# Delta-rule block with a routed expert layer, one core: the gate's columns inside the experts' operand, products of a pair in three parts, and other list orders in the last stage

## Chip, cores and metric

The kernel runs on one NeuronCore of a Trainium2 chip. The metric is the device time of one execution in microseconds, lower is better. Three executions of the kernel before took 234.13, 236.33 and 236.86 us, median 236.33.

## The reference

The input x is 4 x 1024 x 128 in float32. The program adds two sublayers to it, each on a layer-normalised copy of x:

```python
# sublayer 1, on layernorm(x): delta rule over the 1024 positions, then an MLP
qkv = x @ gates_w + gates_b; q, k, v = split(qkv, 3); k = k / norm(k)
u = solve_triangular(tril(k k^T, -1) + I, v); y = (q k^T) @ (lr * u)
h = x + y @ out_w + out_b
h = h + relu(layernorm(h) @ w1 + b1) @ w2 + b2
# sublayer 2, on layernorm(x1): one of 8 experts a row, by the largest score
scores = x @ gate_w.T; chosen = argmax(scores)        # 8 scores a row
x = x + expert_w[chosen] @ x                           # expert_w: 8 x 128 x 128
```

The normalisation ahead of sublayer 2 is folded into the operands: gate and expert weights are centred once, so that they can be applied to x1 itself, and the factor 1/std of each row is applied to the chosen result afterwards. The scores of a row differ from the true ones only by that positive factor, which changes no argmax.

## The kernel before, in words

Positions are cut into T = 8 tiles of 128 rows; each tile holds all NS = 4 sequences. Each engine has one program-ordered list, and semaphores join them. The first two thirds of the span compute k, v, the triangular solve and the state; the last stage, from about 125 us on, goes through the tiles once more with the state known. The change is nearly all in this stage. For a tile t its steps are:

- `delta` (TensorE) multiplies q's operand with the state into PSUM bank 0; `h2_` (VectorE) adds it to h; `xb_` (GpSimd) adds h to x; `hstats`, `haggr` (VectorE: one statistics and one aggregate instruction a sequence), `hroot` (ScalarE, square root), `hscale`, `hbias` (VectorE) give the normalisation; `tn_` (ScalarE, four instructions) applies it.
- `tT_`, `hid_`, `out_` (TensorE, banks 1, 2, 2) with their evacuations `tT_` and `hid_` on ScalarE are the MLP; `x1_` (VectorE) adds its result to x.
- `x1T_` transposes the sum (TensorE, bank 1) and evacuates it (ScalarE). `gate` multiplies each transposed block with the 8 centred score columns `gwC` into bank 3: four matmuls of 8 columns. `choose` (VectorE) takes the maximum of the 8 scores and compares, which makes the mask, for four sequences at once.
- `experts(t, pair, half)` (TensorE) multiplies the blocks of a pair of sequences with four experts, 512 columns of `ewC`, one bank a sequence: half 0 (experts 0 to 3) goes to banks 4 and 5, half 1 to 6 and 7. `default` (ScalarE) copies expert 0's result to `sel`. Seven `pick`s (VectorE, predicated copies of 128 x 256) put experts 1 to 7 in place where the mask says so; each waits for the one before it. A bank is written anew only when the picks that read it are over: half 0 of a pair waits for three picks of the pair before, half 1 for all seven.
- `xstats`, `xaggr`, `xroot`, `xscale` give 1/std of the sum; `scale` (ScalarE) applies it, `add_` (GpSimd) adds the result to x, and SP's queue stores the tile. For the last tile VectorE does the last scaling and adding itself (line 1039).

The lists at the end of each engine's block order all this by hand: while tile t's experts are picked, tile t + 1 is in its MLP, t + 2 in its normalisation and t + 3 in delta. `prep` (lines 427 to 438 and 1091 to 1105) and `expert_` and `expert_one` (1108 to 1115) centre the gate's and the experts' weights during the earlier stages, through bank 4. A float32 matmul shows as two passes in the profile: "x4" for the two matmuls of `experts`.

Of the kernel before, what the change touches and what calls it, by code (L numbers as in the profile page):

```python
# [5 lines left out]
P = 128  # L6
# [3 lines left out]
ALU = mybir.AluOpType  # L10
# [7 lines left out]
def delta_block_kernel(  # L18
# [44 lines left out]
    with ExitStack() as ctx:  # L63
        def sb(name, shape, dtype=F32):
            return ctx.enter_context(nc.sbuf_tensor(name, shape, dtype))

        def sem(name):
            return ctx.enter_context(nc.semaphore(name))
# [6 lines left out]
        def rows(t):  # L75
# [111 lines left out]
        x1T_mm, x1T_ready, gate_mm, max_done, mask_ready = (sem("x1T_mm"), sem("x1T_ready"), sem("gate_mm"),  # L187
                                                            sem("max_done"), sem("mask_ready"))
# [13 lines left out]
        AHEAD = 1  # L202

# [145 lines left out]
        def _(act):  # L349
# [77 lines left out]
            def prep(j):  # L427
                act.wait_ge(prep_mm, j + 1)
                if j == 0:
                    nc.scalar.copy(wqT[:], ps[:, 4, 0:C])  # L430
                    last = nc.scalar.copy(gwT[:], ps[:, 4, C:C + E])
                elif j == 3:
                    last = nc.scalar.copy(gwC[:], ps[:, 4, 0:E])
                else:
                    q = (j - 1) % 3
                    last = nc.scalar.copy((ewT if j < 3 else ewC)[:, EH * q:EH * q + EH, :].rearrange("p e f -> p (e f)"),
                                          ps[:, 4, :])
                last.then_inc(prep_ready, 1)
# [219 lines left out]
            for t in range(T):  # L658
                if 0 < t < T - 1:
                    tT_(t + 1)  # L660
                if t + 2 < T:
                    tn_(t + 2, LOW)
                default(t, 0)
                if t + 1 < T:
                    hid_(t + 1)
                if t + 2 < T:
                    tn_(t + 2, HIGH)
                if t > 0:
                    scale(t - 1)
                xroot(t)  # L670
                default(t, 1)
                if t + 1 < T:
                    x1T_(t + 1)
                if t + 3 < T:
                    hroot(t + 3)

        @block.vector
        def _(dve):
# [267 lines left out]
            def choose(t, of=ALL):  # L946

                scores = ps[:, 3, 0:NS * E].rearrange("p (n e) -> p n e", n=NS)[:, span(of)]
                dve.wait_ge(gate_mm, upto(t, of))
                nc.vector.tensor_reduce(mx[t % 2][:, span(of)], scores, AX_X, ALU.max).then_inc(max_done, len(of))  # L950
                dve.wait_ge(max_done, upto(t, of))
                nc.vector.tensor_tensor(mask[t % 2][:, span(of)], scores,
                                        mx[t % 2][:, span(of)].unsqueeze(2).broadcast_to([P, len(of), E]),
                                        ALU.is_equal).then_inc(mask_ready, len(of))

            def pick(t, pair, j):

                e = j + 1
                half = e // EH
                b = 4 + 2 * half  # L960
                n = slice(2 * pair, 2 * pair + 2)
                if j == 0:
                    dve.wait_ge(mask_ready, NS * t + 2 * pair + 2)
                    dve.wait_ge(default_set, 2 * t + pair + 1)
                else:
                    dve.wait_ge(picked, (E - 1) * (2 * t + pair) + j)
                if j == 0 or e == EH:
                    dve.wait_ge(ex_mm, 4 * t + 2 * pair + half + 1)
                nc.vector.copy_predicated(  # L969
                    sel[t % 2][:, n], mask[t % 2][:, n, E - 1 - e].unsqueeze(2).broadcast_to([P, 2, F]),  # L970
                    ps[:, b:b + 2, (e % EH) * F:(e % EH) * F + F]).then_inc(picked, 1)
# [19 lines left out]
            choose(0, LOW)  # L991
            hstats(2)
            haggr(2)
            choose(0, HIGH)
            for t in range(T):
# [3 lines left out]
                if t > 0:  # L999
                    choose(t)  # L1000
# [12 lines left out]
                if far:  # L1013
                    hstats(t + 3, LOW)
# [30 lines left out]
        def _(pe):  # L1045
# [265 lines left out]
            def gate(t, of=ALL):  # L1311
                pe.wait_ge(x1T_ready, upto(t, of))
                earlier(pe, mask_ready, NS * t + of[0])
                for n in of:
                    last = nc.tensor.matmul(ps[:, 3, n * E:n * E + E], x1T[t % 2][:, n], gwC[:], start=True, stop=True)  # L1315
                last.then_inc(gate_mm, len(of))

            def experts(t, pair, half):
                i = 2 * t + pair
                pe.wait_ge(x1T_ready, NS * t + 2 * pair + 2)  # L1320

                earlier(pe, picked, (E - 1) * i - (EH if half == 0 else 0))
                for n in range(2):
                    last = nc.tensor.matmul(ps[:, 4 + 2 * half + n, :], x1T[t % 2][:, 2 * pair + n],  # L1324
                                            ewC[:, EH * half:EH * half + EH, :].rearrange("p e f -> p (e f)"),
                                            start=True, stop=True)
                last.then_inc(ex_mm, 1)
# [60 lines left out]
```

## Time and profile before

| | |
|---|---|
| runs | 234.13, 236.33, 236.86 us |
| profiled execution | 233.88 us, span 232.1 us |
| TensorE (PE) | 203.6 us busy, 88% |
| VectorE (DVE) | 164.5 us, 71% |
| ScalarE (ACT) | 122.8 us, 53% |
| GpSimd (POOL) | 58.9 us, 25% |
| line 1324, the experts' matmuls | 128 passes, 60.4 us busy |
| line 969, the picks | 112 instructions, 48.9 us busy |
| line 1315, the gate's matmuls | 64 passes |

The span is the time from the first to the last instruction; the execution's own time is a little longer. Busy time is that of one engine, and passes of matmuls overlap in it, so that the spacing of their starts says more than their durations. PEld is the loading of the stationary operand, which overlaps the matmul before it. PEclk is the granted TensorE clock as a share of 2.4 GHz. The last stage ends at 232.1; its tile steps are 11.4 us apart in the middle and 10.3 towards the end.

### The profile page before, as it was taken

The page shows a single profiled execution, that of the slowest core. Times are in us where ns is not written, and L with a number is a line of the kernel's source. Part 1 is how long each engine was busy: PE and PEld are TensorE (multiplying, and loading weights), DVE is VectorE, ACT ScalarE, POOL GpSimd, SP SyncE. Part 2 cuts the span into 40 slices and gives each one's busy share as a digit, 9 for nine tenths or more (in the row PEclk, how much of TensorE's full clock was granted, in tenths as well). Part 3 has the DMA queues.
Part 4 walks back from the last instruction along what each step waited for, and adds up shares of the span by engine and source line. Part 5 has one row for each costly group of instructions (what it writes and reads, how often), then busy time and mean ns, then how long its engine had stood idle before and what let it go on. Part 6 is the DMA issues. An engine that isn't in the chain of part 4 may idle for free.

```text
span 232.1 us, 4284 instructions
## 1 busy us (share of the span) xinstructions
PE 203.6 (88%) x1347; PEld 146.6 (63%) x1347; DVE 164.5 (71%) x748; ACT 122.8 (53%) x324; POOL 58.9 (25%) x73
## 2 busy tenths in 40 slices
PE   0795988999999759999989498999999999999980
PEld 0454666977799658989987285565656565565520
DVE  7994999999489854142353825969696878787785
ACT  2585565789585652434672555354646373735130
POOL 7255800000000069740200402206060606022020
PEclk9999799999999975557999859999999999999998
DMA  5951011000000000000000000001010101010111
GB/s 137 265 138 26 3 24 21 6 3 0 3 4 0 3 0 0 4 0 0 4 0 3 1 0 0 0 3 47 0 45 1 48 1 45 0 45 3 45 47 45
DMA packets 15612, 5.92 MB, mean 26 GB/s; under 512 B 5468, under 2 KB 15590, under 8 KB 15590
## 3 DMA queue, kind: packets, MB, share of 16 engines
q1 hardware_dynamic: 15014, 5.58, 9.6%
q8 instruction: 11, 0.18, 0.3%
q10 hardware_dynamic: 576, 0.07, 0.2%
q14 instruction: 11, 0.09, 0.1%
HBM read 3.09 MB, written 2.10 MB: 22 GB/s over the span
## 4 chain that ended last, share of the span: by engine, by line
PE 72%; DVE 8%; ACT 5%; issue 3%; DVEq 0%; ACTq 0%
PE ps L1324 22%; PE ps L1053 8%; PE ps L1048 5%; PE ps L1220 4%; PE ps L1224 4%; PE ps L1214 4%; PE ps L1232 3%; PE ps L1080 3%; PE ps L1299 3%; PE ps L1315 3%; PE ps L1150 2%; PE ps L1160 2%; DVE kT_all L969 2%; PE ps L1124 2%; ACT tt_all L448 1%
## 5 line engine op out<-in xcount | busy, mean ns | idle before, releaser
L1324 PE MATMUL ps<-ewC,kT_all 128*128 128x512 f32 x128 | 60.4, 596 | 0.9 <-DVE kT_all L969 0.8
L969 DVE COPY_PREDICATED kT_all<-mask,ps 128x256 f32<-128x256 int32 x112 | 48.9, 436 | 17.2 <-ACT kT_all L634 11.1
L1324 PEld LDWEIGHTS ps<-ewC,kT_all 128*128 128x128 f32 x128 | 22.0, 190 | 19.2 <-issue 19.2
L315 POOL TENSOR_SCALAR h_all<-x_all,mv,rr 128x128 f32<-128x128 f32 x16 | 12.4, 790 | 54.9 <-DVE da_all L817 54.9
L333 POOL TENSOR_TENSOR x_all<-x_all,kT_all 128x512 f32<-128x512 f32 x7 | 8.9, 1270 | 55.4 <-ACT kT_all L640 55.4
L789 DVE TENSOR_TENSOR xi<-xi,prod 128x60 f32<-128x60 f32 (+13 forms) x116 | 19.5, 207 | 0.3
L782 DVE TENSOR_TENSOR prod<-lts,xi 128x60 f32<-128x60 f32 (+13 forms) x116 | 19.3, 206 | 0.3
L328 POOL TENSOR_TENSOR x_all<-x_all,h_all 128x512 f32<-128x512 f32 (+1 forms) x9 | 10.3, 1147 | 30.9 <-DVE h_all L900 24.1
L611 ACT ACTIVATE k_all<-h_all,nb,rr 128x128 f32<-128x128 f32 x32 | 14.0, 484 | 4.2 <-DVE nb L921 4.2
L839 DVE SCALAR_TENSOR_TENSOR rv<-v_all,nk,ps 128x128 f32<-128x128 f32 x28 | 8.4, 345 | 10.0 <-PE ps L1214 9.5
L1048 PE MATMUL ps<-ident,h_all 128*128 128x128 f32 x32 | 6.0, 320 | 9.4 <-ACT h_all L363 7.0
L634 ACT COPY kT_all<-ps 128x256 f32<-128x256 f32 x16 | 5.8, 363 | 15.6 <-PE ps L1324 15.6
L1048 PEld LDWEIGHTS ps<-ident,h_all 128*128 128x128 f32 x32 | 4.7, 168 | 14.9 <-issue 14.6
L299 POOL TENSOR_SCALAR h_all<-x_all,mv,rr 128x128 f32<-128x128 f32 x14 | 11.1, 804 | 10.6 <-DVE rr L710 10.6
L322 POOL TENSOR_TENSOR x_all<-x_all,b2s 128x512 f32<-128x512 f32 x8 | 10.1, 1268 | 12.0 <-ACT h_all L527 12.0
L1220 PE MATMUL ps<-rv,tt_all 128*128 128x128 f32 x64 | 10.9, 323 | 1.4 <-DVE tt_all L832 0.6
L1053 PE MATMUL ps<-kT_all 128*128 128x128 f32 x64 | 9.9, 303 | 2.3 <-ACT kT_all L372 2.3
L1053 PEld LDWEIGHTS ps<-w2s,k_all 128*128 128x128 f32 x64 | 9.2, 208 | 4.0 <-issue 3.3
L1053 PEld LDWEIGHTS ps<-kT_all 128*128 128x128 f32 x64 | 8.4, 205 | 4.5 <-ACT kT_all L372 4.4
L1053 PEld LDWEIGHTS ps<-gg_all,xnT_all 128*128 128x128 f32 x64 | 9.1, 209 | 3.0 <-issue 2.4
L1220 PEld LDWEIGHTS ps<-rv,tt_all 128*128 128x128 f32 x64 | 9.4, 225 | 2.1 <-DVE rv L839 1.4
L1315 PEld LDWEIGHTS ps<-gwC,kT_all 128*128 128x128 f32 x64 | 8.5, 193 | 3.3 <-issue 3.3
(160 smaller groups left out, 437.4 us busy)
## 6 DMA issues: line engine op xcount, KB each, us to landing
x_all<-in_L_attn_x_dram SPq DMA_DIRECT2D x7, 256.0 KB, 5.5
out_dram<-x_all SPq DMA_DIRECT2D x7, 256.0 KB, 2.3
ew<-in_L_ffn_expert_w_dram SPq DMA_DIRECT2D x1, 512.0 KB
gd<-gg_all SPq DMA_DIRECT2D x28, 16.0 KB, 1.8
x_all<-in_L_attn_x_dram SPq DMA_DIRECT2D x2, 128.0 KB, 2.6
out_dram<-x_all SPq DMA_DIRECT2D x2, 128.0 KB, 1.8
wall<-in_L_attn_gates_w_dram SPq DMA_DIRECT2D x2, 64.0 KB
wall<-in_L_attn_gates_w_dram ACTq DMA_DIRECT2D x1, 64.0 KB, 2.6
```

The source lines that it names most:

```text
L299: nc.gpsimd.tensor_scalar(xh[:, t, n], x_all[:, t, n], mv[:, 0, t, n, 0:1], rr[:, t, 1, n:n + 1], ALU.subtract, ALU.mult).then_inc(xh_pool, 1)
L315: last = nc.gpsimd.tensor_scalar(h_all[:, t, n], x_all[:, t, n], mv[:, 0, t, n, 0:1], rr[:, t, 0, n:n + 1], ALU.subtract, ALU.mult)
L328: nc.gpsimd.tensor_tensor(x_all[:, t, span(of)], x_all[:, t, span(of)], h_all[:, t, span(of)], ALU.add).then_inc(xb_ready, len(of))
L611: nc.scalar.activation(tn[t % 2][:, n], h_all[:, t, n], ACT.Identity, bias=nb2[:, t, n:n + 1], scale=rr2[:, 0, t, n:n + 1]).then_inc(tn_re ...
L782: nc.vector.tensor_tensor(mul[half], lts[:, j, lo:hi].unsqueeze(2).broadcast_to([P, hi - lo, w]), xi[g][:, j, 0:w].unsqueeze(1).broadcast_ ...
L789: nc.vector.tensor_tensor(xi[g][:, lo:hi, 0:w], xi[g][:, lo:hi, 0:w], mul[half], ALU.subtract).then_inc(elim, 1)
L969: nc.vector.copy_predicated(sel[t % 2][:, n], mask[t % 2][:, n, E - 1 - e].unsqueeze(2).broadcast_to([P, 2, F]), ps[:, b:b + 2, (e % EH) * ...
L1048: last = nc.tensor.transpose(tiles(bank)[:, n], src(n), ident[:])
L1053: last = nc.tensor.matmul(tiles(bank)[:, n], lhsT(n), rhs(n), start=True, stop=True)
L1220: nc.tensor.matmul(ps[:, n, C:2 * C], tt_all[:, t, n], rv[:, n], start=True, stop=True).then_inc(w_mm, 1)
L1315: last = nc.tensor.matmul(ps[:, 3, n * E:n * E + E], x1T[t % 2][:, n], gwC[:], start=True, stop=True)
L1324: last = nc.tensor.matmul(ps[:, 4 + 2 * half + n, :], x1T[t % 2][:, 2 * pair + n], ewC[:, EH * half:EH * half + EH, :].rearrange("p e f -> ...
```

## The change

`gwC` is gone. `ewC` is now one row of 8 x 128 + 8 columns: experts 0 and 1, the 8 score columns, experts 2 to 7. A pair's products come in three parts of 256, 392 and 384 columns (`COLS`). Part 0 puts both sequences side by side in bank 3; part 1, with the scores, goes to banks 4 and 5; part 2 to 6 and 7. The matmuls `gate` are removed; `choose` works on a pair and waits for part 1, twice a tile. The waits of `experts` follow the picks that free each bank: 1, 4 or 7 of the pair before. In `prep`, the centred weights are evacuated to their new places, one of them in two copies. The lists of the stage are reordered:

- TensorE: tT_, part 0, hid_, part 1, delta, part 2, out_, then the second pair's parts 0 and 1, x1T_, part 2.
- ScalarE: default comes ahead of tn_, which is now one block of four behind hid_; hroot(t + 2) follows default(t, 0) instead of hroot(t + 3) at the end of the step.
- VectorE: hstats(t + 3) and haggr(t + 3), which stood between the picks, follow the last pick of the step.

```diff
-        gwT, gwC = sb("gwT", [P, E]), sb("gwC", [P, E])
+        gwT = sb("gwT", [P, E])
-        ewT, ewC = sb("ewT", [P, E, F]), sb("ewC", [P, E, F])
+        ewT, ewC = sb("ewT", [P, E, F]), sb("ewC", [P, E * F + E])
+        COLS = (slice(0, 2 * F), slice(2 * F, 5 * F + E), slice(5 * F + E, 8 * F + E))
...
+        def expert(e):
+            if e < 2:
+                return ps[:, 3, :].rearrange("p (n c) -> p n c", n=2)[:, :, e * F:e * F + F]
+            if e < 5:
+                return ps[:, 4:6, E + (e - 2) * F:E + (e - 1) * F]
+            return ps[:, 6:8, (e - 5) * F:(e - 4) * F]
...
@@ ScalarE: prep @@
-                    last = nc.scalar.copy(gwC[:], ps[:, 4, 0:E])
+                    last = nc.scalar.copy(ewC[:, 2 * F:2 * F + E], ps[:, 4, 0:E])
...
+                elif j == 4:
+                    nc.scalar.copy(ewC[:, 0:2 * F], ps[:, 4, 0:2 * F])
+                    last = nc.scalar.copy(ewC[:, 2 * F + E:4 * F + E], ps[:, 4, 2 * F:4 * F])
                 else:
...
+                    last = nc.scalar.copy(ewC[:, 4 * F + E:8 * F + E], ps[:, 4, :])
@@ ScalarE: default and the list @@
-                act.wait_ge(ex_mm, 4 * t + 2 * pair + 1)
+                i = 2 * t + pair
+                act.wait_ge(ex_mm, 3 * i + 1)
                 earlier(act, added, t - 1)
-                nc.scalar.copy(sel[t % 2][:, 2 * pair:2 * pair + 2], ps[:, 4:6, 0:F]).then_inc(default_set, 1)
+                nc.scalar.copy(sel[t % 2][:, 2 * pair:2 * pair + 2], expert(0)).then_inc(default_set, 1)
...
             for t in range(T):
                 if 0 < t < T - 1:
                     tT_(t + 1)
-                if t + 2 < T:
-                    tn_(t + 2, LOW)
                 default(t, 0)
+                if 0 < t < T - 2:
+                    hroot(t + 2)
                 if t + 1 < T:
                     hid_(t + 1)
                 if t + 2 < T:
-                    tn_(t + 2, HIGH)
+                    tn_(t + 2, ALL)
                 if t > 0:
                     scale(t - 1)
                 xroot(t)
                 default(t, 1)
                 if t + 1 < T:
                     x1T_(t + 1)
-                if t + 3 < T:
-                    hroot(t + 3)
@@ VectorE: choose, pick and the list @@
+            def choose(t, pair):
+                i = 2 * t + pair
+                of = slice(2 * pair, 2 * pair + 2)
+                scores = ps[:, 4:6, 0:E]
+                dve.wait_ge(ex_mm, 3 * i + 2)
+                nc.vector.tensor_reduce(mx[t % 2][:, of], scores, AX_X, ALU.max).then_inc(max_done, 1)
+                dve.wait_ge(max_done, i + 1)
+                nc.vector.tensor_tensor(mask[t % 2][:, of], scores, mx[t % 2][:, of].unsqueeze(2).broadcast_to([P, 2, E]),
+                                        ALU.is_equal).then_inc(mask_ready, 1)
...
-                if j == 0 or e == EH:
-                    dve.wait_ge(ex_mm, 4 * t + 2 * pair + half + 1)
+                if e == 5:
+                    dve.wait_ge(ex_mm, 3 * i + 3)
...
-                if t > 0:
-                    choose(t)
+                choose(t, 0)
                 if ahead:
                     hbias(t + 2)
                 pick(t, 0, 0)
...
                 pick(t, 0, 4)
-                if far:
-                    hstats(t + 3, LOW)
                 pick(t, 0, 5)
                 if nxt:
                     x1_(t + 1)
                 pick(t, 0, 6)
-                if far:
-                    hstats(t + 3, (2,))
+                choose(t, 1)
                 pick(t, 1, 0)
-                if far:
-                    hstats(t + 3, (3,))
                 pick(t, 1, 1)
-                if far:
-                    haggr(t + 3, LOW)
                 pick(t, 1, 2)
                 xscale(t)
                 pick(t, 1, 3)
-                if far:
-                    haggr(t + 3, HIGH)
                 pick(t, 1, 4)
                 pick(t, 1, 5)
                 pick(t, 1, 6)
+                if far:
+                    hstats(t + 3)
+                    haggr(t + 3)
@@ TensorE @@
-            def gate(t, of=ALL):
...
-            def experts(t, pair, half):
+            def experts(t, pair, third):
                 i = 2 * t + pair
                 pe.wait_ge(x1T_ready, NS * t + 2 * pair + 2)
-                earlier(pe, picked, (E - 1) * i - (EH if half == 0 else 0))
+                earlier(pe, picked, (E - 1) * (i - 1) + (1, 4, 7)[third])
+                of = COLS[third]
+                w = of.stop - of.start
                 for n in range(2):
-                    last = nc.tensor.matmul(ps[:, 4 + 2 * half + n, :], x1T[t % 2][:, 2 * pair + n],
...
+                    dst = ps[:, 3, n * w:n * w + w] if third == 0 else ps[:, 2 + 2 * third + n, 0:w]
+                    last = nc.tensor.matmul(dst, x1T[t % 2][:, 2 * pair + n], ewC[:, of], start=True, stop=True)
                 last.then_inc(ex_mm, 1)
...
             delta(2)
-            gate(0, LOW)
             x1T_(0, HIGH, 6)
             experts(0, 0, 0)
-            tT_(1)
-            gate(0, HIGH)
             for t in range(T):
-                if 0 < t < T - 1:
+                if t + 1 < T:
                     tT_(t + 1)
                 if t > 0:
                     experts(t, 0, 0)
                 if t + 1 < T:
                     hid_(t + 1)
+                experts(t, 0, 1)
                 if t + 3 < T:
                     delta(t + 3)
-                experts(t, 0, 1)
+                experts(t, 0, 2)
                 if t + 1 < T:
                     out_(t + 1)
                 experts(t, 1, 0)
+                experts(t, 1, 1)
                 if t + 1 < T:
                     x1T_(t + 1)
-                experts(t, 1, 1)
-                if t + 1 < T:
-                    gate(t + 1)
+                experts(t, 1, 2)
```

## Rows read from the trace of the kernel before

**Rows 1.** Busy time by stretch: engines, PEclk (granted clock), DMA share, GB/s.
```profile
85.00:96.90 11.90, 11.90 (x94) 10.80 (x92) 3.55 (x11) 3.20 (x11) 11.90 (x16) 0.50 0.00 0
152.21:163.57 11.36, 11.36 (x52) 6.82 (x52) 9.05 (x39) 6.09 (x15) 3.77 (x3) 1.00 0.09 25
218.35:232.10 13.75, 7.59 (x18) 2.77 (x17) 9.53 (x32) 2.21 (x7) 1.27 (x1) 0.95 0.14 39
```

**Rows 2.** The chain of waits, t = 2: start, us, what.
```profile
164.21 1.72 PE ps L1324 x4
165.93 0.86 PE ps L1299 x2
166.78 0.89 PE ps L1053 x8
...
174.29 0.79 PE ps L1315 x8
```

**Rows 3.** Timeline of TensorE: the transposes of four tiles at x1T_.
```profile
149.16 0.66 PE L1048 MATMUL ps<-ident,x_all 128*128 128x128 f32 x4 [0.32 <-DVE x_all L927]
...
194.62 0.65 PE L1048 MATMUL ps<-ident,x_all 128*128 128x128 f32 x4
...
205.05 0.60 PE L1048 MATMUL ps<-ident,x_all 128*128 128x128 f32 x4
...
215.39 0.60 PE L1048 MATMUL ps<-ident,x_all 128*128 128x128 f32 x4
```

**Rows 4.** Timeline of VectorE, t = 0 and 1: start, us, line, operation, idle.
```profile
139.83 0.86 DVE L906 BATCH_NORM_STATS2 st<-h_all 128x6 f32<-128x128 f32 x4
140.73 0.38 DVE L912 BATCH_NORM_AGGREGATE mv<-st 128x2 f32<-128x6 f32 x4
...
142.71 0.18 DVE L917 RECIPROCAL rr<-sd 128x4 f32<-128x4 f32 x1 [0.26 <-ACT sd L600]
...
153.53 0.16 DVE L950 TENSOR_REDUCE mx<-ps 128x4 f32<-128x32 f32 x1
153.79 0.19 DVE L952 TENSOR_TENSOR mask<-ps,mx 128x32 int32<-128x32 f32 x1
...
155.32 0.45 DVE L969 COPY_PREDICATED kT_all<-mask,ps 128x256 f32<-128x256 int32 x1 [1.26 <-ACT kT_all L634]
155.66 0.48 DVE L933 BATCH_NORM_STATS2 st<-x_all 128x6 f32<-128x128 f32 x2
156.05 0.43 DVE L969 COPY_PREDICATED kT_all<-mask,ps 128x256 f32<-128x256 int32 x1
...
158.48 0.37 DVE L939 BATCH_NORM_AGGREGATE mv<-st 128x2 f32<-128x6 f32 x4
...
159.79 0.68 DVE L927 TENSOR_TENSOR x_all<-ps,x_all 128x512 f32<-128x512 f32 x1
160.39 0.44 DVE L969 COPY_PREDICATED kT_all<-mask,ps 128x256 f32<-128x256 int32 x1
```

**Rows 5.** Timeline of ScalarE: an evacuation of ewC, and the stage's start.
```profile
59.23 0.59 ACT L436 COPY ewC<-ps 128x512 f32<-128x512 f32 x1
...
141.64 0.78 ACT L617 ACTIVATE k_all<-ps,cols 128x512 f32<-128x512 f32 x1 [1.79 <-PE ps L1048]
142.32 0.29 ACT L600 ACTIVATE sd<-mv,epsc 128x4 f32<-128x4 f32 x1
```

**Rows 6.** Timeline of TensorE and of VectorE round the first tile.
```profile
138.61 0.51 PE L1315 MATMUL ps<-gwC,kT_all 128*128 128x8 f32 x4
...
144.41 0.45 DVE L969 COPY_PREDICATED kT_all<-mask,ps 128x256 f32<-128x256 int32 x1 [1.26 <-ACT kT_all L634]
```

**Rows 7.** Timeline of VectorE, the end of the program.
```profile
220.81 0.44 DVE L969 COPY_PREDICATED kT_all<-mask,ps 128x256 f32<-128x256 int32 x1 [0.75 <-ACT kT_all L634]
...
226.93 1.87 DVE L969 COPY_PREDICATED kT_all<-mask,ps 128x256 f32<-128x256 int32 x4 [0.17 <-PE ps L1324]
228.69 1.13 DVE L1039 SCALAR_TENSOR_TENSOR x_all<-kT_all,rr,x_all 128x128 f32<-128x128 f32 x4
```

More of the change, by code:

```diff
@@ L186, in delta_block_kernel @@
         hid_mm, hid_ready, out_mm, x1_ready = sem("hid_mm"), sem("hid_ready"), sem("out_mm"), sem("x1_ready")
-        x1T_mm, x1T_ready, gate_mm, max_done, mask_ready = (sem("x1T_mm"), sem("x1T_ready"), sem("gate_mm"),
-                                                            sem("max_done"), sem("mask_ready"))
+        x1T_mm, x1T_ready, max_done, mask_ready = (sem("x1T_mm"), sem("x1T_ready"), sem("max_done"),
+                                                   sem("mask_ready"))
         xst_done, xmv_done, xsd_done, xrr_done = sem("xst_done"), sem("xmv_done"), sem("xsd_done"), sem("xrr_done")
@@ L432, in prep @@
                 elif j == 3:
-                    last = nc.scalar.copy(gwC[:], ps[:, 4, 0:E])
-                else:
-                    q = (j - 1) % 3
-                    last = nc.scalar.copy((ewT if j < 3 else ewC)[:, EH * q:EH * q + EH, :].rearrange("p e f -> p (e f)"),
-                                          ps[:, 4, :])
+                    last = nc.scalar.copy(ewC[:, 2 * F:2 * F + E], ps[:, 4, 0:E])
+                elif j < 3:
+                    last = nc.scalar.copy(ewT[:, EH * (j - 1):EH * j, :].rearrange("p e f -> p (e f)"), ps[:, 4, :])
+                elif j == 4:
+                    nc.scalar.copy(ewC[:, 0:2 * F], ps[:, 4, 0:2 * F])
+                    last = nc.scalar.copy(ewC[:, 2 * F + E:4 * F + E], ps[:, 4, 2 * F:4 * F])
+                else:
+                    last = nc.scalar.copy(ewC[:, 4 * F + E:8 * F + E], ps[:, 4, :])
                 last.then_inc(prep_ready, 1)
@@ L944, in xscale @@
                 nc.vector.reciprocal(rr2[:, 1, t], sd2[:, 1, t]).then_inc(xrr_done, 1)
[L946 to L954, printed above, removed]
+            def choose(t, pair):
[7 more added lines that the diff above has]
+                                        ALU.is_equal).then_inc(mask_ready, 1)
@@ L956, in pick @@
             def pick(t, pair, j):
-                e = j + 1
-                half = e // EH
-                b = 4 + 2 * half
+                e, i = j + 1, 2 * t + pair
                 n = slice(2 * pair, 2 * pair + 2)
                 if j == 0:
-                    dve.wait_ge(mask_ready, NS * t + 2 * pair + 2)
-                    dve.wait_ge(default_set, 2 * t + pair + 1)
-                else:
-                    dve.wait_ge(picked, (E - 1) * (2 * t + pair) + j)
-                if j == 0 or e == EH:
-                    dve.wait_ge(ex_mm, 4 * t + 2 * pair + half + 1)
+                    dve.wait_ge(mask_ready, i + 1)
+                    dve.wait_ge(default_set, i + 1)
+                else:
+                    dve.wait_ge(picked, (E - 1) * i + j)
@@ L990, in _ @@
             h2_(2)
-            choose(0, LOW)
             hstats(2)
             haggr(2)
-            choose(0, HIGH)
             for t in range(T):
@@ L1309, in x1T_ @@
                 turn(bank, lambda n: x_all[:, t, n], x1T_mm, of, len(of))
-            def gate(t, of=ALL):
[L1312 to L1316, printed above, removed]
-            def experts(t, pair, half):
+            def experts(t, pair, third):
                 i = 2 * t + pair
                 pe.wait_ge(x1T_ready, NS * t + 2 * pair + 2)
-                earlier(pe, picked, (E - 1) * i - (EH if half == 0 else 0))
+                earlier(pe, picked, (E - 1) * (i - 1) + (1, 4, 7)[third])
+                of = COLS[third]
+                w = of.stop - of.start
                 for n in range(2):
-                    last = nc.tensor.matmul(ps[:, 4 + 2 * half + n, :], x1T[t % 2][:, 2 * pair + n],
-                                            ewC[:, EH * half:EH * half + EH, :].rearrange("p e f -> p (e f)"),
-                                            start=True, stop=True)
+                    dst = ps[:, 3, n * w:n * w + w] if third == 0 else ps[:, 2 + 2 * third + n, 0:w]
+                    last = nc.tensor.matmul(dst, x1T[t % 2][:, 2 * pair + n], ewC[:, of], start=True, stop=True)
                 last.then_inc(ex_mm, 1)
```

2 lines of the change are left out of this document (1 added, 1 removed).

## The prediction

> **What bounds the kernel now.** I read the busy time by stretch first. In a full tile step of the last stage, 152.21 to 163.57, TensorE is busy for 11.36 of 11.36 us at PEclk 1.00, the upper level (2.4 GHz); VectorE for 9.05, ScalarE for 6.09 [rows 1]. The chain of waits then says whose time a step is: from the second tile on it runs through TensorE instructions alone, end to end, until the last tile [rows 2], so a microsecond taken from TensorE there is a microsecond of the program, as long as nobody else needs more. The timeline shows the rhythm: the x1T_ transposes of tiles 1, 5, 6 and 7 start at 149.16, 194.62, 205.05 and 215.39 [rows 3]. That is (194.62 - 149.16)/4 = 11.365 us per step for four steps, then 10.43 and 10.34 where delta has run out, then 228.69 + 1.13 - 215.39 = 14.43 us to VectorE's last instruction [rows 7], a part in which TensorE is busy for only 7.59 of 13.75 us [rows 1]. VectorE's slack in a step is small: 1.26 us before the first pick [rows 4] and about 1 us in small pieces.
>
> **TensorE's side of the change.** The gate is 0.79 us a step for 8 passes, 0.099 each, though 8 columns wide; an experts' matmul is 4 passes for two tiles, 1.72/4 = 0.430 for 512 columns, and 0.89/8 = 0.111 for 128 [rows 2]. Between these lie (0.430 - 0.111)/384 = 0.00083 us a column. The three parts of 256, 392 and 384 columns cost then 0.217, 0.330 and 0.324 a pass, four passes each: 0.87, 1.32 and 1.29 us, 3.48 a pair. Before, a pair was 3.44; the step pays 0.08 more for the experts and saves 0.79: 0.70 net, with rounding, to 10.67 us. So far as TensorE goes, the gate's weight loads vanish beneath columns that were computed anyway. Bounds for the unseen widths: 0.87 could be 0.89 (eight 128-column passes) and no less than its columns; small.
>
> **VectorE's side.** It gets a second choose per step and loses fillers between its picks. From [rows 4]: pick, two statistics, pick is 156.05 - 155.32 = 0.73, in which the statistics start 0.34 after the pick. A pick behind a pick must wait for it: four of them last 1.87, so one starts (1.87 - 0.44)/3 = 0.48 after the other [rows 7]. An h2_ or x1_ in between costs 0.33 + 0.60 = 0.93 (160.39 - 159.79 = 0.60), four aggregates 0.33 + 0.28 = 0.61 (their 0.37 less the overlap). Reduce to mask is 0.26 (153.53 to 153.79). Mask to the first pick directly behind it is in no row: it lies between the 0.19 of the mask alone and 0.30; I take 0.26, as for the pair just named. One step in the new order:
> - first pair, pick 0 to pick 6: 0.73 + 0.73 + 0.93 (h2_) + 0.61 + 0.48 + 0.93 (x1_) = 4.41
> - pick 6, second choose, pick: 0.33 + 0.26 + 0.26 = 0.85
> - second pair, six chained gaps: 6 x 0.48 = 2.88 (xscale fits into one)
> - tail and head: 0.33; four statistics and the wait for them 140.73 - 139.83 = 0.90; four aggregates 0.38; then the root on ScalarE, 0.29 [rows 5], with a hand-over of 0.10 either way (142.61 to 142.71), as nothing stands between haggr(t + 3) and the next step's hscale any more: 0.49; hscale's issue 0.09; reduce and mask 0.52: 2.71.
>
> Sum 10.85 us, against TensorE's 10.67. So **VectorE becomes the bound**, by a little, and a step saves 11.365 - 10.85 = 0.51 and not 0.70. Of the saving on TensorE, 0.19 turns into its waiting for x1_ and for picks. The 1.26 us before the first pick is gone as a wait: it came from default(t, 0) queued on ScalarE behind tn_, and default now goes first; tn_ as one block of four is late by less than the 6 us until tT_ of the step after wants it. hroot on ScalarE stands behind default(t, 0), which needs part 0: from the end of x1_ on, TensorE gets there in 0.54 + 1.29 + 0.54 + 0.87 = 3.24 us and the default is over by 3.7, while VectorE ends its aggregates at 0.25 + 0.52 + 2.88 + 0.33 + 0.90 + 0.38 = 5.3. So the root goes at once, with 1.6 us to spare. POOL and SP keep their lists.
>
> **Step by step.**
> - First tile: gate(0, LOW) at 138.61 goes [rows 6]. The transposes start there (0.16 for the pass still draining), then 0.27, 0.87 and 0.54 for tT_(1): 140.45. tT_'s evacuation on ScalarE is 0.78 [rows 5], with 0.10 of hand-overs 141.33; hid_ 0.86 and part 1 with 1.32: 143.51; 0.10 and choose 0.52: first pick at 144.13, before 144.41 [rows 6]. To x1_(1): 0.73 + 0.73 + 0.93 + 0.61 + 0.48 + 0.33 = 3.81, its own 0.68, hand-over 0.05: x1T_(1) at 148.67 and not 149.16 [rows 3]: **0.49**.
> - Four steps of 0.51: **2.06**. Bounds: 0 (VectorE at 11.365) and 4 x 0.70 = 2.8.
> - Tile 5 to 6: no h2_ in it (-0.45), 10.40 against 10.43: **0.03**.
> - Tile 6 to 7: no statistics. TensorE alone would need 9.65, but one loop is longer: transposes 0.54 (0.66 [rows 3] less the 0.12 in which the next already runs), last part 1.29, tT_ 0.54, part 0 0.87, hid_ 0.86, part 1 1.32 = 5.42; 0.10 + choose 0.52; picks to x1_ 3.03 + 0.33; x1_ 0.68 + 0.05: 10.13. Against 10.34: **0.21**.
> - Last tile, from x1T_(7): 0.54 + 1.29 + 0.87 + 1.32 + 0.10 + 0.52 = 4.64 to the first pick; first pair without h2_ and x1_ 3.51, seam 0.85, 2.88, and from the last pick's start to the end 1.45 (229.82 less 226.93 + 3 x 0.48) [rows 7]: 13.33 against 14.43: **1.10**. A late start of pick 0 (a wait of 0.75 [rows 7]) is part of what it gives back.
> - Preparation: one 0.59 evacuation of ewC [rows 5] becomes two of half the width and the other keeps its size. Between 0 and 0.1 on ScalarE; the cover is TensorE, which is in the chain there. I take 0; without the cover 0.1.
>
> Sum: 0.49 + 2.06 + 0.03 + 0.21 + 1.10 = **3.9 us**. The profiled execution took 233.88 (span 232.1), so 230.0; the median of the runs shown, 236.33, lies 2.45 above it, in runs from 234.13 to 236.86. Against the median I forecast **232.4**.
>
> **Rivals.**
> *TensorE stays the bound.* The rows show a statistics instruction starting 0.34 after a pick of 0.45, against 0.48 for a dependent pick [rows 4, 7]; my order has five more dependent gaps per step. If they cost no more than independent ones, VectorE's step is 10.85 - 5 x 0.14 = 10.15, and TensorE's 10.67 holds: 4 x 0.70 + 0.49 + 0.3 + 0.21 + 1.1 = 4.9, so 231.4. The Trainium skill (VectorE: DVE Perf Modes, The DRAIN you can't avoid) has that rule: a semaphore between instructions costs nothing extra, since the pipe empties anyway. The trace disagrees in its 0.34 against 0.48. Chance 0.20.
> *VectorE's step does not get shorter than 11.37.* The seam mask-to-pick, or the root behind default on ScalarE, costs 0.5 more than summed; each stands bare in VectorE's queue. Then only 0.49 + 1.10 and some 0.2 are left: 1.8, 234.5. For it: every piece is taken as its row has it, with nothing for the meeting of two lists, and the two engines now wait for each other twice a pair. Against: rows for all but one piece. Chance 0.28.
> *The clock falls (slower).* TensorE gets pauses of some 0.2 us in every step where it had none. In the stretch 85.00 to 96.90 PEclk is 0.50, the lower level (1.2 GHz) [rows 1], so it happens in this program. One step at that level would take twice TensorE's 10.67, 21.3 us and not 10.85. It decides from about 0.8 of a step on, where 3.9 us of gain and 4.7 of threshold are used up; one whole step is 10.5 - 3.9 = 6.6 us slower, 242.9. Against it: in the last 13.75 us, TensorE busy 7.59, PEclk is still 0.95 [rows 1]. The Trainium skill (TensorE: Matmul & The Clock Gate, A second HAM failure mode) warns of just that, an engine idling briefly between groups of matmuls as it cycles through PSUM; here the trace of before, full at 1.00, can't show it. Chance 0.04.
>
> **How the numbers follow.** Forecast 0.48, the rest as said. The range 229.9 to 235.3 takes in both neighbours (231.4 and 234.5) and about 1 us of scatter between runs, and leaves out the clock case. Two per cent of the median is 4.7 us, about what a measurement of this kernel can tell from no change. Faster by more than that takes most of the first rival (0.11), a third of the forecast's share through scatter (0.17) and a little else: 0.31. Slower by 2%: 0.04. Within: 0.65.
>
> **What would show it.** x1T_ starts 10.85 apart and not 10.67; TensorE with small waits for VectorE (x1_, picks) in every step; VectorE busy near 10 of 10.85 with its longest wait at hscale for the root, about 0.5; no wait for default left; no matmul of 8 columns, and passes of 256 columns at 0.217. Wrong would be: mask to pick far from 0.26, chained picks other than 0.48, default or hroot late on ScalarE, or PEclk under 1.00 after 141 us.

## The result, and the profile after

The changed kernel took 224.98, 225.43, 230.84 and 233.25 us, median 228.13; before 236.19 in the same comparison. The ratio is 0.955, interval 0.945 to 0.965: **faster, by 4.5%** (it leaves out disturbed runs: the changed kernel's two at 231 and 233; of before, all of whose runs were alike, none). The profiled execution took 230.84 (span 229.0) against 233.88: 3.0 us less. Forecast was 232.4, range 229.9 to 235.3, so the measured median lies below the range, while the profile moved by nearly what was summed. Both need an explanation.

TensorE's timeline first: the x1T_ transposes that [rows 3] show for before, here of tiles 1 to 7.

```profile
149.30 0.60 PE L1051 MATMUL ps<-ident,x_all 128*128 128x128 f32 x4
...
160.10 0.60 PE L1051 MATMUL ps<-ident,x_all 128*128 128x128 f32 x4
...
170.90 0.60 PE L1051 MATMUL ps<-ident,x_all 128*128 128x128 f32 x4
...
181.70 0.60 PE L1051 MATMUL ps<-ident,x_all 128*128 128x128 f32 x4
...
192.71 0.66 PE L1051 MATMUL ps<-ident,x_all 128*128 128x128 f32 x4
...
203.01 0.66 PE L1051 MATMUL ps<-ident,x_all 128*128 128x128 f32 x4
...
213.32 0.66 PE L1051 MATMUL ps<-ident,x_all 128*128 128x128 f32 x4
```

Three steps of 10.80, one of 11.01, then 10.30 and 10.31; before they were 11.365 (four), 10.43 and 10.34. The chain of waits of one step (start, us, what), as [rows 2] for before:

```profile
151.19 0.44 PE ps L1051 x4
151.63 0.86 PE ps L1323 x4
152.50 0.10 issue
152.59 1.10 PE ps L1302 x2
153.69 1.32 PE ps L1323 x4
155.01 0.89 PE ps L1056 x8
155.90 1.29 PE ps L1323 x4
```

The gate's 0.79 is gone, and the three parts cost 0.86, 1.32 and 1.29, as summed. The chain is still TensorE from end to end. What it now holds is 0.10 of "issue" ahead of hid_ and 1.10 for two matmuls that took 0.86 in [rows 2]. VectorE's timeline at the turn of the step (the last bracket is the idle time before, and who ended it):

```profile
153.13 0.86 DVE L918 BATCH_NORM_STATS2 st<-h_all 128x6 f32<-128x128 f32 x4
154.03 0.38 DVE L924 BATCH_NORM_AGGREGATE mv<-st 128x2 f32<-128x6 f32 x4
154.90 0.18 DVE L929 RECIPROCAL rr<-sd 128x4 f32<-128x4 f32 x1 [0.49 <-ACT sd L613]
155.04 0.17 DVE L964 TENSOR_REDUCE mx<-ps 128x2 f32<-128x16 f32 x1
155.25 0.17 DVE L966 TENSOR_TENSOR mask<-ps,mx 128x16 int32<-128x16 f32 x1
155.34 0.15 DVE L933 SCALAR_TENSOR_TENSOR nb<-mv,rr 128x4 f32<-128x4 f32 x1
155.46 0.45 DVE L980 COPY_PREDICATED kT_all<-mask,ps 128x256 f32<-128x256 int32 x1
```

And ScalarE's, the evacuation of tT_ and default:

```profile
151.72 0.78 ACT L630 ACTIVATE k_all<-ps,cols 128x512 f32<-128x512 f32 x1 [1.14 <-PE ps L1051]
152.53 0.37 ACT L648 COPY kT_all<-ps 128x256 f32<-128x256 f32 x1
```

The 1.26 before the first pick [rows 4] is gone, and the wait for the root, 0.49, is the one summed. Mask to pick, in no row of before, is 0.21 (155.25 to 155.46), and so is reduce to mask, 0.26 before. ScalarE's evacuation of tT_ ends at 152.50, when part 0 also ends on TensorE: that is what hid_ waits for. The end:

```profile
217.94 0.44 DVE L980 COPY_PREDICATED kT_all<-mask,ps 128x256 f32<-128x256 int32 x1
...
225.65 1.14 DVE L1042 SCALAR_TENSOR_TENSOR x_all<-kT_all,rr,x_all 128x128 f32<-128x128 f32 x4
```

From x1T_(7) to the end 226.79 - 213.32 = 13.47 against 14.43. In all, from tile 1's transposes to the end 77.49 against 80.66.

The other half of the result stands ahead of all this. Busy time by stretch of the changed kernel (us, then PE, PEld, DVE, ACT, POOL busy, PEclk, DMA share, GB/s):

```profile
80.90:84.84 3.94, 0.87 (x25) 0.79 (x26) 2.95 (x6) 2.93 (x6) 1.00 (x2) 0.97 0.00 0
84.84:108.90 24.06, 24.06 (x199) 21.95 (x196) 7.10 (x22) 8.24 (x27) 15.17 (x18) 0.51 0.00 1
```

From 81 to 84.5 TensorE mostly waits, and then it runs for 24 us at half clock. The kernel before did so too, from 84 to 107 (0.50 over these 23 us; [rows 1] shows 85.00 to 96.90 of them). The four runs had mean granted clocks of 0.950 and 0.958 (224.98, 225.43), 0.923 and 0.924 (230.84, 233.25): this stretch is not the same in every execution.

### The profile page after: what moved, and what is told of

It reads as the page before. It is cut to its first block, busy times and chain, and to the rows that moved or that the text cites. A ratio compares the mean times of both kernels' runs of the same rounds, so it can differ in the third digit from the quotient of the medians.

```text
span 229.0 us, 4282 instructions
## 1 busy us (share of the span) xinstructions
PE 199.8 (87%) x1347; PEld 150.9 (66%) x1347; DVE 169.5 (74%) x762; ACT 122.6 (54%) x325; POOL 59.0 (26%) x73
## 4 chain that ended last, share of the span: by engine, by line
PE 72%; DVE 7%; ACT 6%; issue 2%; DVEq 0%; ACTq 0%
PE ps L1323 23%; PE ps L1056 9%; PE ps L1051 5%; PE ps L1223 4%; PE ps L1227 4%; PE ps L1302 4%; PE ps L1217 4%; PE ps L1235 3%; PE ps L1083 3%; PE ps L1153 2%; PE ps L1163 2%; DVE kT_all L980 2%; PE ps L1127 1%; ACT tt_all L461 1%; PE ps L1144 1%
## 5 line engine op out<-in xcount | busy, mean ns | idle before, releaser
L1323 PE MATMUL ps<-ewC,kT_all 128*128 128x256 f32 (+2 forms) x192 | 62.0, 455 | 0.7 <-DVE kT_all L980 0.7
L1323 PEld LDWEIGHTS ps<-ewC,kT_all 128*128 128x128 f32 x192 | 33.9, 190 | 17.2 <-issue 6.6
L624 ACT ACTIVATE k_all<-h_all,nb,rr 128x128 f32<-128x128 f32 x32 | 13.4, 484 | 3.5 <-DVE nb L933 3.5
L1302 PE MATMUL ps<-k_all,w1s 128*128 128x512 f32 (+1 forms) x18 | 9.5, 614 | 2.4 <-issue 1.0
L641 ACT COPY kT_all<-ps 128x512 f32<-128x512 f32 (+1 forms) x9 | 4.8, 537 | 12.0 <-PE ps L1051 12.0
L630 ACT ACTIVATE k_all<-ps,cols 128x512 f32<-128x512 f32 (+1 forms) x9 | 6.6, 730 | 8.7 <-PE ps L1051 8.7
L838 DVE TENSOR_SCALAR tt_all<-ps 32x128 f32<-32x128 f32 x4 | 1.2, 289 | 13.3 <-PE ps L1144 13.3
```

The costliest lines, as they stand in the source:

```text
L624: nc.scalar.activation(tn[t % 2][:, n], h_all[:, t, n], ACT.Identity, bias=nb2[:, t, n:n + 1], scale=rr2[:, 0, t, n:n + 1]).then_inc(tn_re ...
L1302: nc.tensor.matmul(rows(tiles(bank)[:, span(of)]), w1s[:], rows(tT[t % 2][:, span(of)]), start=True, stop=True).then_inc(hid_mm, len(of))
L1323: last = nc.tensor.matmul(dst, x1T[t % 2][:, 2 * pair + n], ewC[:, of], start=True, stop=True)
```

## Experiments

Twelve kernels in three groups of four (e1 to e4, e5 to e8, e9 to e12), each group on a chip of its own, beside new runs of the kernel before. A comparison across groups, as e6 or e11 with e4, is one across chips.

**e1: the change again.**

> The changed kernel as it is. Its profile is 3.0 us shorter than that of before, but its four times spread from 224.98 to 233.25, with mean granted clocks 0.95 to 0.958 in the two short ones and 0.923 to 0.924 in the two long ones. Theory A (the change is worth about 3.5 us and the rest is chance: an execution either has a long stretch at PEclk 0.50 from 84 to 108 us or not, whatever the kernel): runs of the kernel before split in the same way, and at equal clock the two kernels differ by 3 to 4 us. Theory B (the change moves the program out of that stretch): before has no run with a clock over 0.94, the changed kernel has them in about half of its runs, and the ratio stays near 0.955.

Its runs: 224.91, 224.94, 225.41, 225.68, 232.86, 233.15. Before: 228.37, 228.46, 234.18, 234.19 and seven from 235.94 to 236.74. So the kernel before has short executions too, and over all three groups (41 runs) 13 of them, at 228.4 to 229.3; the rest stand at 233.7 to 234.7 and 235.9 to 237.3. The changed kernel has the same three kinds 3.3 to 3.6 us lower: 225.2, 230.8, 233.1 on average (the middle one is a single run). **Theory A**: at equal clock the change is worth 3.4 us, and the ratio of this group, which now has short runs on both sides, is 0.986 (0.983 to 0.990); 4.7 of the 8.1 between the first medians is which kind was drawn (two short ones of four, against none of four).

The upper two kinds have the same mean clock (0.923 to 0.924) and lie 2.3 us apart, so the low stretch does not tell them apart. The profile of this group fell on a run of 232.86. It runs behind that of the 230.84 long before the low stretch: by 0.85 at the transposes at 22.20 (23.05 here), and by 2.47 at the last matmuls ahead of TensorE's pause (profile of 230.84, then of 232.86):

```profile
79.76 1.06 PE L1235 MATMUL ps<-k_all,ww 128*128 128x128 f32 x8
...
82.23 1.06 PE L1235 MATMUL ps<-k_all,ww 128*128 128x128 f32 x8
```

At tile 1's transposes it is 2.01 behind (151.31 against 149.30), and the ends of the spans are 2.1 apart. So an execution has a start, **early** or **late** by 2 to 3 us, and a low stretch, short or long. The profiles of before, e3, e5, e7, e9, e10 and e11 have these matmuls at 79.35 to 80.05, those of e2, e4, e6 and e12 at 82.2 to 82.7; where a kernel's runs stand in two groups 2 to 3 us apart, the late profile belongs to the upper group and the early one to the lower. What makes a start late was not tested.

**e7 and e8: the only difference ahead of the low stretch**, one evacuation of ewC in two copies.

```diff
 e7, on the kernel before:
+                elif j == 4:
+                    nc.scalar.copy(ewC[:, 0:2, :].rearrange("p e f -> p (e f)"), ps[:, 4, 0:2 * F])
+                    last = nc.scalar.copy(ewC[:, 2:4, :].rearrange("p e f -> p (e f)"), ps[:, 4, 2 * F:4 * F])
 e8, on the changed kernel:
-                    nc.scalar.copy(ewC[:, 0:2 * F], ps[:, 4, 0:2 * F])
-                    last = nc.scalar.copy(ewC[:, 2 * F + E:4 * F + E], ps[:, 4, 2 * F:4 * F])
+                    last = nc.scalar.copy(ewC[:, 0:2 * (2 * F + E)].rearrange("p (a c) -> p a c", a=2)[:, :, 0:2 * F],
+                                          ps[:, 4, :].rearrange("p (a c) -> p a c", a=2))
```

> The kernel before, but one 128x512 evacuation of ewC at about 59 us in two halves, as in the change. It is the only difference between the two kernels ahead of the low stretch. Of the runs of the kernel before so far 2 of 15 were short (228.4), of the changed kernel's 6 of 10 (225). If the copy decides, about half of these six runs are short ones at 228.4; if it is chance, no more than one or two are.

> The changed kernel with both halves of that evacuation in one instruction (a destination of two pieces). If the copy decides whether the low stretch is short, this kernel's runs are mostly long ones (233) like those of before; if it is chance, or something else of the change, they split as the changed kernel's did. Otherwise the time is the changed kernel's to within 0.1 us.

e7 had 6 short runs of 12, and the kernel before, beside it, 6 of 17; at equal clock the ratio is 1.000 (0.9985 to 1.0018), so the second copy costs nothing. e8: 225.39, 225.74, 230.76, 233.09, 233.26, and one execution at 287.45 whose granted clock was 0.655 over the whole of it, left out. Short runs: 8 of 16 for the changed kernel and e8, 13 of 45 for before with its first four. That is not enough to say that the change moves the odds, nor that it doesn't; the copy does not decide it. The profile of e7 fell on a short run and shows what is short in it:

```profile
84.84:94.80 9.96, 9.96 (x82) 9.15 (x83) 3.55 (x11) 2.87 (x10) 9.96 (x14) 0.52 0.00 0
94.80:108.90 14.10, 13.93 (x178) 12.69 (x177) 6.16 (x22) 9.72 (x33) 6.67 (x7) 0.98 0.01 3
```

The fall comes at the same place, but the clock is back after 10 us and not after 24, with TensorE busy throughout in both.

**e4 and e5: TensorE's pause filled**, in the changed kernel and in before. The products are not used.

```diff
+            def fill(k):
+                for _ in range(k):
+                    nc.tensor.matmul(ps[:, 7, 0:C], ident[:], ident[:], start=True, stop=True)
...
                 if t + 1 == TG:
+                    fill(9)
                     ya(t + 1)
+                    fill(4)
```

> The changed kernel with 13 idle matmuls of 128x128 by ident into a free part of PSUM, in TensorE's two pauses of 2.12 and 1.03 us around 81 to 84 us, ahead of the stretch at PEclk 0.50. Their result is not used. If the pauses bring the granted clock down, PEclk stays 1.00 from 84 to 108 us, every run has a mean clock of about 0.95 or more and takes 225 us or less. If the fall has another cause, the runs split as the changed kernel's own, and the matmuls cost 0 to 0.5 us.

> The kernel before with the same 13 idle matmuls in the pauses at 81 to 84 us (their result is not used). If the long stretch at PEclk 0.50 is all that splits the runs, this kernel has one kind of run too, its steps are 11.365 us, and it stands to the changed kernel with the filler (221.28) as the two kernels do at equal clock: 3.2 us longer, 224.5. If the change had a second effect outside the last stage, the distance would be another: 8 us by the first medians.

e4: 220.55 to 222.93, median 221.28; e5: 224.09 to 227.08, median 225.59. No run is left in either with a mean clock under 0.973, and e4's trace, of a late start, with the filled pauses at 83.1 to 87.1, has no low stretch there:

```profile
80.60:84.84 4.24, 3.68 (x34) 3.61 (x33) 3.96 (x15) 2.83 (x10) 0.00 (x0) 1.00 0.02 4
84.84:108.90 24.06, 23.68 (x320) 21.42 (x319) 11.08 (x39) 15.34 (x49) 17.42 (x20) 1.00 0.01 2
```

So the pause brings this fall, and the fall's length makes the short and the long runs. The two groups that are left, 220.6 and 222.8 in e4, 224.3 and 227.0 in e5, are early and late starts. At the same start the filler is worth 4.6 us against a short run and 10 against a long one (e4: 220.6 against 225.2 and 230.8). Between the two filled kernels the change is worth 3.6 us (means of their lower three runs, early starts: 220.6 and 224.3) or 4.2 (late starts, 222.8 and 227.0; e4's run of 221.81, whose clock of 0.982 is another, is in neither): a cleaner measure of the change than the first medians, though the two ran on different chips.

**e3 and e2: one half of the change each.** e3 is the kernel before with the new lists on ScalarE and VectorE; e2 is the new operand, with its three parts and TensorE's new list, and the old lists on ScalarE and VectorE.

```diff
 e2, on the changed kernel (e3 is the reverse, on the kernel before):
+                if t + 2 < T:
+                    tn_(t + 2, LOW)
                 default(t, 0)
-                if 0 < t < T - 2:
-                    hroot(t + 2)
...
-                    tn_(t + 2, ALL)
+                    tn_(t + 2, HIGH)
...
+                if t + 3 < T:
+                    hroot(t + 3)
 ... and on VectorE hstats(t + 3), haggr(t + 3) between the picks again
```

> The gate and the two halves of before, but ScalarE's and VectorE's lists in the new order. Theory of the prediction (TensorE bound in before, 11.365 us a step): nothing or a little worse, as TensorE still has the gate's 0.79 us a step: 11.3 to 11.5 us a step and the tail up to 0.5 us shorter since default comes earlier. Rival (the orders give the gain): 1 to 3 us faster than before.

> The gate's columns in the experts' operand and the three parts, but ScalarE's and VectorE's lists in the order of before (statistics of tile t + 3 between the picks, tn_ LOW ahead of default, hroot(t + 3) at the end of the step). If the picks' order limits the step, VectorE has fillers in the chained gaps and no bare wait for the root, but default and the second choose wait longer: tn_ LOW ahead of default costs about 0.9 on ScalarE before the first pick, so a step of 11.2 to 11.5 us and a profile 2 to 3 us longer than the changed kernel's. If TensorE alone set the time, the step would be 10.67 and the profile 0.5 us shorter than the changed kernel's.

e3 takes what before takes, as expected: 228.41 for a short run (before: 228.4 to 229.3), 11.26 a step (one of 11.54). e2 is slower, 237.76 to 245.05, and its step is 12.94, far over the 11.2 to 11.5 expected. Its timeline:

```profile
168.74 0.30 ACT L613 ACTIVATE sd<-mv,epsc 128x4 f32<-128x4 f32 x1 [1.61 <-DVE mv L926]
168.94 0.76 ACT L630 ACTIVATE k_all<-ps,cols 128x512 f32<-128x512 f32 x1
...
169.80 1.10 PE L1310 MATMUL ps<-k_all,w1s 128*128 128x512 f32 x2 [0.73 <-issue]
...
172.25 0.17 DVE L966 TENSOR_REDUCE mx<-ps 128x2 f32<-128x16 f32 x1 [2.25 <-PE ps L1331]
...
172.74 0.88 ACT L624 ACTIVATE k_all<-h_all,nb,rr 128x128 f32<-128x128 f32 x2 [3.04 <-DVE nb L935]
173.53 0.35 ACT L648 COPY kT_all<-ps 128x256 f32<-128x256 f32 x1
...
173.98 0.44 DVE L982 COPY_PREDICATED kT_all<-mask,ps 128x256 f32<-128x256 int32 x1 [1.27 <-ACT kT_all L648]
```

It is a ring. The scores come with part 1 and so choose waits for TensorE; hbias stands behind choose on VectorE, tn_ waits for hbias, default stands behind tn_ on ScalarE and the first pick waits for default. And hroot(t + 3), late itself, holds up tT_'s evacuation, hid_ and part 1. The new operand is a loss without new lists beside it.

**e11: which of the two orders.** The changed kernel with the filler and VectorE's old list.

> The changed kernel with the filler, ScalarE in the new order, VectorE in the order of before. With both orders of before the step was 12.94: there ScalarE ran hroot(t + 3) ahead of tT_'s evacuation, hid_ waited 0.73 for it, and default stood behind two tn_. If ScalarE's order is what the new operand needs, this kernel is back at 10.6 to 10.9 us a step, 220.5 to 222 in all. If VectorE's order matters as much, its step lies between 11.5 and 12.9.

Median 222.31, steps of 11.00 (one of 11.33): 0.20 above the changed kernel's 10.80, with VectorE waiting 1.61 for part 1. So ScalarE's order takes the step from 12.94 to 11.00, and VectorE's is worth 1.0 us in all (221.28 to 222.31). VectorE's new order with ScalarE's old one was not run.

**e12: what the gate's price is.** Before with the filler, gates 64 columns wide.

```diff
-                    last = nc.tensor.matmul(ps[:, 3, n * E:n * E + E], x1T[t % 2][:, n], gwC[:], start=True, stop=True)
+                    last = nc.tensor.matmul(ps[:, 3, n * 64:n * 64 + 64], x1T[t % 2][:, n], gwC[:], start=True, stop=True)
```

> The kernel before with the filler, and gates 64 columns wide (56 of them zero) instead of 8. If a pass of the gate is bound by loading its stationary operand, 64 columns cost as little as 8: by the slope, 64 columns are 0.058 us a pass, below the 0.099 measured, so the step stays at 11.365 and the time at 225.6. If its price followed the columns, each step would gain 8 x 56 x 0.00083 = 0.37 us and the time would be 228.5.

Steps of 11.36 to 11.38, times 223.97 to 227.17: no change. Eight passes take 0.84 in the chain (below), 0.05 more than with 8 columns, and the transposes behind them are 0.04 shorter than the 0.49 of before. Up to 64 columns the price is that of a pass and not of what it multiplies. That the loading of its 128 columns of stationary operand sets this price fits, but no run takes the loading apart from the rest of a pass.

```profile
167.56 0.84 PE ps L1322 x8
168.40 0.45 PE ps L1049 x4
```

**e6: who bounds the changed step.**

```diff
+                experts(t, 0, 1)
                 if t + 1 < T:
                     hid_(t + 1)
-                experts(t, 0, 1)
```

> The changed kernel with the filler, and hid_(t + 1) behind part 1 on TensorE instead of ahead of it. In the profile of the changed kernel TensorE waits at hid_ for the evacuation of tT_ in every step (0.10 in the chain, and 1.10 for matmuls that take 0.86 when nothing is waited for). If that wait is what makes the step 10.80 and not 10.67, the step becomes 10.67 and the last three steps, which wait for part 1, get 0.3 to 0.6 shorter: 219.5 to 220.7 against 221.28. If VectorE's own list were the bound, the step would stay at 10.80: its choose comes earlier but its work is the same.

Median 219.51; steps of 10.60 (three), 10.91, 10.14, 9.65. At the same start the gain is 2.3 us (lower three runs, 218.3 against 220.6). The wait at hid_ was the bound: 0.20 a step goes with it, more than the 0.13 expected, which was reckoned from a TensorE sum that e9 shows to be too high. In VectorE's timeline a step now has no wait but this one, so its own list should be the bound now; e9 tests it:

```profile
156.47 0.18 DVE L929 RECIPROCAL rr<-sd 128x4 f32<-128x4 f32 x1 [0.49 <-ACT sd L613]
```

**e9: VectorE's list.** e6 with the statistics in the second pair's gaps.

```diff
                 pick(t, 1, 0)
+                if far:
+                    hstats(t + 3, (0,))
 ... (1,), (2,), (3,) behind picks 1, 3 and 4, haggr(t + 3) behind pick 5
-                if far:
-                    hstats(t + 3)
-                    haggr(t + 3)
```

> The changed kernel with the filler and hid_ behind part 1, and with the statistics and aggregates of tile t + 3 in the chained gaps of the second pair instead of behind the last pick. In the profile of the kernel without this, VectorE has no wait in a step of 10.60 but 0.49 for the root. If VectorE's list is the bound there, it gets about 1.4 us shorter (0.90 + 0.38 + 0.49 gone, 0.37 paid between the picks) and the step falls to TensorE's own sum, 2 x 3.47 + 0.86 + 2 x 0.89 + 2 x 0.44 = 10.46: 0.14 for each of five steps, 218.7 against 219.5. If TensorE is the bound already, nothing changes.

Median 217.20, steps of 10.46, all four: TensorE's own sum to the hundredth. VectorE waits 0.88 for it at the second choose. The medians differ by 2.3 and not by 0.8, but three of e6's six runs are late starts and only the upper one or two of e9's; between early starts (218.3 and 217.1) it is 1.3. Beyond the 0.8 there are the last steps, 9.57, and that of 10.91, which is gone.

**e10: the second pause.** e9 with 7, 3 and 3 more idle matmuls between delta(1), tT_, hid_ and tT_ of the first tile.

```diff
             delta(1)
+            fill(7, 5)
             tT_(0, LOW)
+            fill(3, 5)
             hid_(0, LOW)
+            fill(3, 5)
             tT_(0, HIGH, 6)
```

> The kernel with the statistics between, and 13 more idle matmuls in TensorE's pauses of 1.78, 0.81 and 0.27 us at the start of the last stage, ahead of the stretch of some 8 us at PEclk 0.50 (124 to 131 us there). If the pauses bring that stretch too, it is gone and its work of about 6 us takes 1 to 2.5 us less: 216.5 to 217.5, and the two groups of runs (218.2 and 220.3) become one. If not, or if the idle matmuls delay the transposes, 218.7 to 219.5.

214.93 to 215.34, median **215.05**, against 233.99 of before beside it. The low stretch at the start of the stage is gone. Busy time by stretch, nine microseconds of e9, with its pauses:

```profile
122.00:131.00 9.00, 8.06 (x34) 6.35 (x35) 4.12 (x17) 4.63 (x12) 1.05 (x2) 0.62 0.00 0
```

The same nine in e10, PEclk 1.00 in place of 0.62:

```profile
122.00:131.00 9.00, 8.17 (x46) 6.32 (x47) 5.35 (x26) 5.86 (x15) 1.86 (x2) 1.00 0.00 0
```

The six runs agree within 0.2%. The one profiled has the early start; the second filler comes long after the place where early and late part, so that six early starts in a row may be chance. This is the best version: 8% under before's median, and 6.1% (ratio 0.939, 0.938 to 0.941) under its short runs. Of these 13.7 us (228.8 to 215.1), by the means of short runs and then by early starts, the change is 3.6, the first filler 4.6, hid_ 2.3, the statistics 1.3 and the second filler 2.0.

## Why the prediction was wrong

**The step that failed first is the last one: from the profile to the median.** The profiled execution was forecast at 230.0 and took 230.84. I then put the median where before's was, 2.45 higher, with "about 1 us of scatter between runs"; it came out 2.7 below the profile, at 228.13. The scatter is three kinds of execution, 2.3 to 7.9 us apart, and the 2.45 was the distance between two of them: the profile of before was an early start (234.2 on average), the median a late one (236.5), both with the long stretch. The sign was in the rows: a stretch at PEclk 0.50 [rows 1], on which I wrote a rival about new pauses while I took the old stretch as given. That the two profiles, 233.88 and 230.84, were of the same kind, early and long, is luck; without it the step by step below could not be read so. With kinds at 225.2, 230.8 and 233.1, a median of four can be anything between 225 and 233. By the 3.4 us at equal clock the change is 1.4 to 1.5% faster, not 4.5; the rest is the draw.

**Step by step, in the profile.** (The last stage began 0.41 later in the profile after, VectorE's first copy at 124.92 against 124.51; this is taken off. The difference is there at 79 us already, 79.76 against 79.35, and 0.32 of it at 18 us, 18.05 against 17.73, ahead of every instruction that was changed.)
- Gate off TensorE, experts in three parts: forecast 0.217, 0.330, 0.324 a pass, measured 0.86/4 = 0.215, 0.330, 0.323. Right. That the gate pays for a pass and not for its columns: shown by e12, up to 64 columns.
- First tile: forecast 0.49, measured 149.16 - (149.30 - 0.41) = 0.27. Pick 0 came at 144.66 - 0.41 = 144.25 and not 144.13, and the transposes only 0.18 after x1_ had ended (149.12), behind the second pair's part 1 on TensorE.
- Four steps: forecast 2.06, measured 45.46 - 43.41 = 2.05. The size is right and **the reason is not**. "VectorE becomes the bound" is refuted: the chain stays on TensorE, and moving one TensorE instruction (e6) made the step shorter. The step that failed here is an overlap put at nothing, the evacuation of tT_ behind part 0. Two errors cancelled. TensorE's sum without waits is 10.46 (e9), not 10.67, as transposes that wait for nothing take 0.44; and hid_ waits for tT_'s evacuation, since only part 0, 0.86 us, stands between tT_ and hid_ where 1.72 stood before. The wait of 0.10 and the 1.10 in place of 0.86 are the 0.34 from 10.46 to 10.80. I listed tT_, part 0 and hid_ as neighbours and did not set 0.78 of evacuation, with its hand-overs, against 0.86. VectorE's sum of 10.85 was 0.2 too high (0.21, not 0.26, four times): 10.65, and e6, where VectorE bounds, has 10.60. So VectorE came second, by 0.20. Most signs named for it came true all the same (9.94 us busy in a step, a bare wait of 0.49 for the root as its longest, no wait for default): they don't tell which engine bounds.
- One step of the four lasted 11.01: pick 0 started 0.29 late behind its own mask, with nothing in the trace that released it. It is no chance: e1, e4, e6, e9, e10 and e11 have the same 0.29 at the same tile, and nowhere else (in e9 and e10 it costs the step nothing, as VectorE has time there). Why is open.
- Tile 5 to 6 and 6 to 7: forecast 0.03 and 0.21, measured 0.13 and 0.03. Small, 0.16 in all against 0.24. The loop through part 1 and choose that I priced at 10.13 is there and takes 10.31: with hid_ out of it (e6) the last step is 9.65.
- Last tile: forecast 1.10, measured 0.96.
- Preparation at 0: right (e7, 1.000).

Sum: 3.44 measured against 3.9.

**The rivals.** "TensorE stays the bound" was true in its name, but not for its reason nor in its number: dependent picks do cost 0.48 (1.87 for four in the profile after as well). e9 puts a statistics instruction into such a gap, and the pick behind it starts only 0.54 after the one before (159.99 to 160.53). By that the rule of the Trainium skill (VectorE: DVE Perf Modes, The DRAIN you can't avoid), that a semaphore costs nothing between instructions, is not borne out here; the instructions behind the pick differ, though, and no run has the same pair with and without the semaphore. "VectorE's step does not get shorter" fell. The clock rival, new pauses bringing new falls, did not occur: PEclk is 1.00 in every full step of the changed kernel, with 0.10 to 0.11 of TensorE's time idle in each, half of the 0.2 that was forecast. What the Trainium skill (TensorE: Matmul & The Clock Gate, A second HAM failure mode) warns of is not seen at this length of pause. The clock was the right place to look all the same, one stage earlier.

## What to carry to other kernels

Before forecasting a median from a profile, compare its time and clock with those of the other runs, and look for stretches at the lower granted clock and for the pause of TensorE ahead of them: their length can differ from one execution to the next, and then two medians of four runs compare draws. Fill such a pause with idle matmuls in both kernels and compare again, like kind with like. A small product with its own stationary operand costs a pass (the same for 8 and for 64 columns here), so append its columns to a wide one; but then it arrives with the wide one, and every list that had it early must be reordered. When work is taken from between two instructions of one engine, the second of which waits for another engine's copy of the first one's result, set what is left against that copy.

## What was not expected of the hardware

- After a pause of 2.1 and 1.0 us around 82 us, with TensorE busy for 0.87 of 3.94, PEclk fell to 0.50 and stayed there for 10 us in some executions and 24 in others, though TensorE was busy all that time (9.96 of 9.96 and 24.06 of 24.06 us). Nothing in the traces says which it will be.
- A pause of 2.13 us around 21 us was followed by PEclk 0.63 over the next 3.8 us in one profile of the changed kernel (230.84), and by 1.00 over the next 2.85 us in another (232.86), where the fall came behind the next pause, of 1.97 us, at 28 us. So a pause of this length can bring a fall and need not.
- One execution of 287.45 us had 0.655 as its mean granted clock, with steps of 15.7 to 15.8 us. It came once in some 125 executions; why is open.
